# First expert layer: routing weights repeated over the partitions by transfers from a table in memory instead of by TensorE

## What is computed

```python
scores = jax.nn.sigmoid(x @ router_w.T)                 # 2048 tokens x 16 experts
_, topk_idx = jax.lax.top_k(scores + e_bias[None, :], TOP_K)   # TOP_K = 4
topk_w = jnp.take_along_axis(scores, topk_idx, axis=1)
topk_w = topk_w / (topk_w.sum(axis=-1, keepdims=True) + 1e-20)
combine = zeros((T, E)).at[arange(T)[:, None], topk_idx].add(topk_w)
# for each expert, with its column c of combine:
gu = x @ gu_w.T; g, u = jnp.split(gu, 2, axis=1)
acc + c[:, None] * (jax.nn.silu(g) * u @ d_w.T)
# and one shared expert without a weight
```

## Time and profile before

| | |
|---|---|
| median of 3 runs | 739.35 us |
| lowest, highest | 735.06, 740.98 us |
| time of the profiled execution | 740.54 us |
| its span in the profile | 738.8 us |
| mean granted clock of TensorE in it | 0.941 |

### The profile page before, as it was taken

One profiled execution on the slowest core, in us unless ns is written; L12 is line 12 of the kernel. 1 busy time (PEld: TensorE's weight loads), 2 busy tenths in 40 slices (PEclk: granted clock), 3 DMA queues, 4 the chain that ended last, 5 costly groups with the idle time before them and its releaser, 6 DMA issues.

```text
span 738.8 us, 14867 instructions
## 1 busy us (share of the span) xinstructions
PE 694.2 (94%) x4707; PEld 622.9 (84%) x4707; DVE 471.8 (64%) x1331; ACT 257.4 (35%) x484; POOL 356.1 (48%) x435
## 2 busy tenths in 40 slices
PE   4899999999999999998999984899999999999996
PEld 3758878888888888886677773799999999999995
DVE  4958597677777777775799958344544454454443
ACT  1355512333333333346466622222222232323221
POOL 6217693455446545549222034255354655465553
PEclk9786599999999999999899985899999999999999
DMA  9900103678877787769900047422425445434222
GB/s 220 343 3 1 58 0 122 236 247 271 264 242 257 262 265 248 248 230 430 367 20 31 31 138 267 147 44 41 154 45 151 97 122 155 151 75 135 44 37 22
DMA packets 60266, 114.96 MB, mean 156 GB/s; under 512 B 15185, under 2 KB 29394, under 8 KB 57778
## 3 DMA queue, kind: packets, MB, share of 16 engines
q1 hardware_dynamic: 50514, 103.48, 41.0%
q0 software_dynamic: 8736, 10.39, 8.5%
q10 hardware_dynamic: 960, 0.33, 0.2%
HBM read 68.89 MB, written 45.29 MB: 155 GB/s over the span
## 4 chain that ended last, share of the span: by engine, by line
PE 84%; DVE 10%; issue 3%; ACT 2%; DMA 1%; POOLq 0%; POOL 0%; DVEq 0%
PE ps L1114 19%; PE ps L1115 19%; PE ps L1116 19%; PE ps L1399 4%; PE ps L1244 2%; PE ps L1253 2%; PE ps L986 2%; PE ps L1290 2%; PE ps L1050 2%; PE ps L1041 2%; PE ps L1161 1%; PE ps L1266 1%; PE ps L1201 1%; PE ps L1378 1%; PE ps L1282 1%
## 5 line engine op out<-in xcount | busy, mean ns | idle before, releaser
L604 POOL TENSOR_TENSOR part_lo<-wexp,part_hi 128x256 fp32r<-128x256 f32 x136 | 104.8, 795 | 107.4 <-ACT part_hi L855 106.6
L715 POOL DMA_INDIRECT out_rows<-vbd,slot_row x39 | 63.3, 1623 | 105.6 <-DVE vbd L1947 74.0
L1114 PE MATMUL ps<-w_hi,x_high 128*128 x312 | 104.6, 335 | 1.1 <-DVE x_low L1952 1.1
L1115 PE MATMUL ps<-up_low,x_high 128*128 x312 | 101.1, 324 | 0.0
L1116 PE MATMUL ps<-w_hi,x_low 128*128 x312 | 101.0, 324 | 0.0
L1968 DVE TENSOR_TENSOR arena<-arena,ps 128x704 f32<-128x704 f32 x39 | 34.6, 888 | 102.5 <-ACT arena L954 102.5
L1114 PE MATMUL ps<-xn_high,gu_high 128*128 (+3 forms) x208 | 90.9, 437 | 0.0
L837 ACT ACTIVATE wexp<-ps 128x512 f32<-128x512 f32 (+1 forms) x52 | 31.1, 599 | 147.1 <-PE ps L1116 147.1
L1115 PE MATMUL ps<-xn_low,gu_high 128*128 (+3 forms) x208 | 81.9, 394 | 0.0
L1116 PE MATMUL ps<-xn_high,gu_low 128*128 (+3 forms) x208 | 81.7, 393 | 0.0
L954 ACT ACTIVATE arena<-ps 128x704 f32<-128x704 f32 x39 | 29.6, 760 | 119.1 <-PE ps L1116 119.1
(11 more groups left out here) (297 smaller groups left out, 1675.1 us busy)
## 6 DMA issues: line engine op xcount, KB each, us to landing
wexp<-in_wexp SPq DMA_DIRECT2D x68, 256.0 KB, 3.4
w_hi_rows<-part_hi SPq DMA_DIRECT2D x68, 256.0 KB, 3.1
w_lo_rows<-part_lo SPq DMA_DIRECT2D x68, 256.0 KB, 2.7
w_hi<-w_hi_rows SPq DMA_DIRECT2D x8, 2048.0 KB, 19.5
up_low<-w_lo_rows SPq DMA_DIRECT2D x8, 1408.0 KB, 6.0
down_low<-w_lo_rows SPq DMA_DIRECT2D x8, 768.0 KB, 8.3
wexp<-in_gu SPq DMA_DIRECT2D x2, 1632.0 KB, 11.2
xn_rows<-arena SPq DMA_DIRECT2D x8, 256.0 KB, 2.1
```

The source lines that it names most:

```text
L604: r = pool.tensor_tensor(part_lo[:, n % 2, some], part_w[:, n % 4, some], part_hi[:, n % 2, some].bitcast(F32), ALU.subtract)
L715: pool.indirect_dma_start(out=out_rows, out_offset=bass.IndirectOffsetOnAxis(ap=slot_row[:, i:i + 1], axis=0), in_=yb[:, i % 2, :], in_off ...
L1114: pe.matmul(out, high, rows_high, start=start, stop=False, skip_group_check=True)
L1115: pe.matmul(out, high, rows_low, start=False, stop=False, skip_group_check=True)
```

## The change

The three-part split and the spreading matmul go. The normalised weights `cw0` (fp32) of a group are transposed by one fp32 transpose into 64 rows (4 tiles of 16 experts), copied to `cT` by ACT, and stored by SP, in four transfers, as a table `cw_rows` of 16 experts by 2048 tokens in memory. For each chunk from 1 on SP issues two transfers, which read the two experts' rows of 512 tokens once for each partition, into one of four buffers `w_spread` in SBUF (256 KB in all for a chunk). DVE's multiplication by the weights waits for them and reads that buffer instead of PSUM. In SP's program the parts' loop is merged with these transfers.

```diff
+        w_spread = [view(wexp, at, 512) for at in (20416, 20928, 4096, 4608)]
+            def store_weights(first, groups):
+                for j in range(4):
+                    sp.dma_start(cw_v[:, first:first + groups, j, :],
+                                 cT[j * E0:(j + 1) * E0, first * P:(first + groups) * P].rearrange(
+                                     "e (g p) -> e g p", p=P)).then_inc(cw_stored, 16)
+
+            def load_weights(n):
+                g, c = n // (C0 - 1), chunk_of(n % (C0 - 1) + 1)
+                if n >= 4:
+                    sp.wait_ge(b_mult, n - 3)
+                sp.wait_ge(cw_stored, 16 * 8 if g else 16 * 4)
+                e = c * P // I0
+                edge = (e + 1) * I0 - c * P
+                for expert, lo, hi in ((e, 0, edge), (e + 1, edge, P)):
+                    sp.dma_start(w_spread[n % 4][lo:hi, :],
+                                 cw_rows[expert, g * 512:(g + 1) * 512].partition_broadcast(hi - lo)).then_inc(w_in[n % 4], 16)
...
+            sp.wait_ge(b_cT, 1)
+            store_weights(0, 1)
+            sp.wait_ge(x_new, XA)
+            for n in range(3):
+                load_part(n)
+            for n in range(3):
+                load_weights(n)
+            for g in range(NG):
+                for q in range(C0):
+                    if g == 0 and q == 10:
+                        sp.wait_ge(b_cT, 2)
+                        store_weights(1, NG - 1)
+                    n = g * (C0 - 1) + q + 2
+                    if q and n < NG * (C0 - 1):
+                        load_weights(n)
+                    for part in range(parts_by(g, q - 1), parts_by(g, q)):
+                        store_part(part)
...
-            pool.memset(spread, 0.0).then_inc(pool_step, 1)
-            v = spread.rearrange("p (e u) -> p e u", e=E0)
-            for part in range(3):
-                pool.wait_ge(pool_step, 10 + part)
-                pool.affine_select(out=v, in_=v, compare_op=ALU.not_equal, fill=1.0, base=-32 * part,
-                                   pattern=[[-1, E0], [0, I0]], channel_multiplier=1).then_inc(pool_step, 1)
...
-            pool.wait_ge(b_c3, 3)
+            pool.wait_ge(b_chosen, 1)
...
+            def copy_weights(first, groups):
+                act.wait_ge(b_turned, first + groups)
+                at = slice(first * P, (first + groups) * P)
+                act.activation(cT[:, at], bank(4)[0:4 * E0, at], ACT.Copy).then_inc(b_cT, 1)
+            copy_weights(0, 1)
...
-                        pe.matmul(bank(4), spread[:, chunk_of(c) * P:(chunk_of(c) + 1) * P], cT[:, bass.ds(g * 512, 512)],
-                                  start=True, stop=True).then_inc(b_spread, 1)
...
+                pe.transpose(bank(4)[0:4 * E0, g * P:(g + 1) * P], cw0[:, 4 * g:4 * g + 4, :].rearrange("p t e -> p (t e)"),
+                             ident[:, :]).then_inc(b_turned, 1)
 
             up0(0, 0, 0)
             pe.wait_ge(b_sig, 1)
+            pe.wait_ge(v_ready, B)
+            turn_weights(0)
             ffn0_group(0, 0)
...
                     if c:
-                        dve.wait_ge(b_spread, g * (C0 - 1) + c)
-                        dve.tensor_tensor(hm0[:, c % 2, :], hm0[:, c % 2, :], bank(4), ALU.mult).then_inc(b_mult, 1)
+                        dve.wait_ge(w_in[(c - 1) % 4], g * (32 * (C0 - 1) // 4) + 32 * ((c - 1) // 4 + 1))
+                        dve.tensor_tensor(hm0[:, c % 2, :], hm0[:, c % 2, :], w_spread[(c - 1) % 4], ALU.mult).then_inc(b_mult, 1)
```

More of the change, by code:

```diff
@@ L355, in program @@
         NG = NT // 4
-        weights5 = bank(5).bitcast(BF16)
-        WEIGHTS_AT = [bank(4).bitcast(BF16)[:, 0:512], weights5[:, 0:512], weights5[:, 512:1024], weights5[:, 0:512]]
+        w_spread = [view(wexp, at, 512) for at in (20416, 20928, 4096, 4608)]
+        w_in, cw_stored = [sem(f"w_in{n}") for n in range(4)], sem("cw_stored")
+        cw_rows = nc.dram_tensor("cw_rows", (E0, NT * P), F32, kind="Internal").ap()
         PIECE = 256
@@ L427, in load_part, with store_part @@
                 sp.dma_start(part_w[:, n % 4, :], w_flat[:, n * PART:(n + 1) * PART]).then_inc(p_in[n % 4], 16)
-            sp.wait_ge(x_new, XA)
-            for n in range(3):
-                load_part(n)
-            for n in range(NPART):
+            cw_v = cw_rows.rearrange("e (g t p) -> e g t p", t=4, p=P)
+            def store_weights(first, groups):
[13 more added lines that the diff above has]
+                                 cw_rows[expert, g * 512:(g + 1) * 512].partition_broadcast(hi - lo)).then_inc(w_in[n % 4], 16)
+            def store_part(n):
                 part = slice(n * PART, (n + 1) * PART)
@@ L1003, in _ @@
             pe.wait_ge(a_routed, 2)
-            pe.matmul(bank(7)[:, 0:NK], ones[0:1, :], brow, start=True, stop=True).then_inc(a_bias, 1)
+            pe.matmul(bank(7)[:, 0:NK], ones[0:1, :], brow, start=True, stop=True).then_inc(a_route, 1)
             def score_sets(b):
@@ L1154, in ffn0_group @@
                 for c in range(C0):
-                    if c:
-                        if k == 0 and c == 1:
-                            pe.wait_ge(b_cT, 1)
-                            pe.wait_ge(pool_step, 13)
-                        else:
-                            pe.wait_ge(b_mult, g * (C0 - 1) + c - 1)
-                        pe.matmul(bank(4), spread[:, chunk_of(c) * P:(chunk_of(c) + 1) * P], cT[:, bass.ds(g * 512, 512)],
-                                  start=True, stop=True).then_inc(b_spread, 1)
                     if c < C0 - 1:
                         up0(g, c + 1, k)
-                        if k == 0 and c == 0:
-                            turn_weights(0)
                         down0(g, c, k)
                     if k == 0 and c == 8:
-                        turn_weights(1)
-                        turn_weights(2)
-                    if k == 0 and c == 10:
-                        turn_weights(3)
+                        for later in range(1, NG):
+                            turn_weights(later)
                     if k and c in (8, 10):
@@ L1176, in turn_weights @@
             def turn_weights(g):
-                pe.wait_ge(b_c3, 6 if g else 3)
-                if g == 3:
-                    pe.wait_ge(b_cT, 3)
-                at = WEIGHTS_AT[g]
-                for j in range(4):
-                    mm = pe.transpose(at[0:96, j * P:(j + 1) * P], c3[:, 4 * g + j, :], identb[:, :])
-                mm.then_inc(b_turned, 1)
+                pe.wait_ge(b_chosen, 2 if g else 1)
+                pe.transpose(bank(4)[0:4 * E0, g * P:(g + 1) * P], cw0[:, 4 * g:4 * g + 4, :].rearrange("p t e -> p (t e)"),
+                             ident[:, :]).then_inc(b_turned, 1)
             up0(0, 0, 0)
             pe.wait_ge(b_sig, 1)
+            pe.wait_ge(v_ready, B)
+            turn_weights(0)
             ffn0_group(0, 0)
             pe.wait_ge(b_low, B)
-            pe.wait_ge(b_cT, NG)
             with pe.Fori(1, NG) as g:
@@ L1642, in _ @@
             chosen_scores(first).then_inc(b_step, 1)
+            dve.wait_ge(b_step, 4)
+            dve.tensor_reduce(sums[:, first], cw0[:, first, :], AX.X, ALU.add).then_inc(b_step, 1)
             dve.wait_ge(b_step, 5)
[L1644 removed]
+            dve.tensor_scalar(sums[:, first], sums[:, first], 1e-20, None, ALU.add).then_inc(b_step, 1)
             dve.wait_ge(b_step, 6)
[L1646 removed]
+            dve.reciprocal(recs[:, first], sums[:, first]).then_inc(b_step, 1)
             dve.wait_ge(b_step, 7)
[L1648 to L1659 removed]
+            normalised(first).then_inc(b_chosen, 1)
             def select_rest(q):
```

87 lines of the change are left out of this document (24 added, 63 removed).

## The result

The changed kernel took 744.84 us (median of 20 runs, 737.52 to 750.86), the kernel before 738.08 beside it (20 runs): a ratio of 1.0091, 95% interval 1.0061 to 1.0121. That is 6.8 us slower, where the forecast was 1.55 us slower; 745 lies in the range of 731 to 748. The profiled execution has a span of 745.8 us against 738.8.

The account below looks back on a forecast made before the run. PE was taken to bound the kernel, busy 210.2 of 211 us from 115 to 326 us. The terms -1.1 + 1.45 - 10.3 + 11.5 = +1.55 us gave 741 us on the median's scale, range 731 to 748.

Parts of the forecast that it names:

- The spreads, -10.3: On PE, 44 spreading matmuls of 0.235 us each go: -10.3 us.
- The port, +11.5: DVE's multiplication, now with two SBUF inputs, takes turns with POOL; PE stalls 0.67 us in 15 two-part chunks: +11.5 in all.
- The ladder: In two-part chunks DVE and POOL take turns, so the second subtraction ends 5.11 us after the silu, 4.67 before.
- Rivals 2 and 5: Port stalls in two-part chunks: 2, only 0.1 us, 729 to 734, chance 0.20; 5, 0.9 us, 746 to 747, chance 0.07.
- The trade of the two: In the chunk loop, saved spreads of -10.3 us against port stalls of +11.5 us come out about even.
- the likeliest case: Rival 1, the even trade of spreads against port stalls in the chunk loop: 736 to 746 us, chance 0.48.
- The hand-over, +1.45: At the stage's start, the first weights go through memory and land at 100.2 us: +1.45 us, between 0 and 5.
- Rival 4: At the stage's start, the hand-over takes 5 us and the clock falls to 1.2 GHz behind the gap: 747, chance 0.13.
- The program's start, -1.1: Without POOL's selects, DVE's first tensor_scalar, which PE waits for, ends about 1.1 us earlier: -1.1, 0 to -1.3.
- The later store, 0: Group 0, chunk 10: table stores hold SP some 3 us, covered by 3 chunks of weights and 3 parts in hand: 0.
- Traffic, hidden: From 115 to 326 us, 44 chunks of 256 KB raise the DMA share from 0.74 to 0.91, still hidden.
- a rival by bytes, 756: Rival 3: repeated reads of one row cost twice a part's bytes, so the DMA queue becomes the bound: 756, chance 0.12.

Follow-up runs that it names:

- Both taken away: Changed kernel with weight transfers of 16 columns instead of 512 from the fifth chunk on, and the multiplication's operand read from PSUM: 726.06 us, 0.9851.
- small loads: Changed kernel with each weight transfer bringing 16 columns instead of 512 from the fifth chunk on, all transfers and waits kept: 739.82 us, 1.000.
- the same edit alone in the kernel before: Kernel before, with POOL building the 0/1 matrix after the first layer's powers instead of before them: 741.38 us, 1.0065.
- the high store first: Changed kernel with weights issued behind each chunk's parts and each high store ahead of the load three parts on: 737.68 us, 1.000.

## Why the prediction was right and where it was not

*The spreads, -10.3.* Both taken away, groups 1 and 2 take 56.5 and 56.1 us instead of 58.5 and 58.6: 2.0 and 2.5 for 12 spreads, 0.17 to 0.21 each, against 0.235. Where nothing else waits the price is exact: the three steps from silu 5 to silu 8 of group 0 take 4.41 us each in the kernel before and 4.18 or 4.19 in the changed one, 0.23 less.

*The port, +11.5.* The difference of the two runs with small loads is 229.6 - 222.3 = 7.3 us by the sums and 11 by the ratios, so the term was right or a little large. The ladder was right to 0.1 us in the chunk above and in 9 more of the 15; 10 x 0.67 = 6.7 us would be its part in that run (an estimate). In the changed kernel itself it is mostly absent: POOL starts late because ACT is late, most multiplications of groups 1 to 3 take 0.69 to 0.9 us and not 1.13, and only 3 of the 15 chunks end beyond 5.0 us after their silu. Without POOL at work the multiplication takes 0.69 us, not the 0.6 of the forecast. Rivals 2 and 5 were bounds on either side and neither came.

*The trade of the two*, even by the forecast (+1.2), was even: 1.000 with small loads. That is why the forecast for the whole was near. That the measured 745 lies in the range is luck for the rest: nothing in the sum or in the 736 to 746 of the likeliest case stands for the loop of the stores, and the part of the range above it was put there for other causes.

*The hand-over, +1.45.* The timeline of the changed kernel, SP, ACT, DVE and one row of PE:

```profile
88.22 0.22 DVE L1631 TENSOR_TENSOR arena<-arena,recs 128x64 f32<-128x64 f32 x1
89.87 1.28 ACT L863 ACT_TABLE_LOAD   x1
89.88 1.71 SPq L430 DMA_DIRECT2D cw_rows<-arena  x4
91.16 0.59 ACT L863 ACTIVATE wexp<-ps 96x512 f32<-96x512 f32 x1
91.63 1.38 SPq L425 DMA_DIRECT2D wexp<-in_wexp  x3
93.05 6.81 SPq L442 DMA_DIRECT2D wexp<-cw_rows  x10
94.02 0.35 PE L1135 MATMUL ps<-dn_high,h_high 96*128 96x256 f32 x1 [1.71 <-DVE h_low L1710]
97.53 1.21 DVE L1701 TENSOR_TENSOR wexp<-wexp 128x512 f32<-128x512 f32 x1 [1.39 <-DMA wexp<-cw_rows]
```

From the normalised weights (88.44) to the first multiplication 9.1 us go by; the forecast had 8.4 (91.8 to 100.2). The way over memory was priced well: the stores landed 1.3 to 1.4 us after their issue and the first two loads 3.6 and 3.9, where the forecast had 2.1 and 3.4. By the fit of the Trainium skill, "DMA: Bandwidth & Descriptors", section "Anatomy of one DMA" (about 2.0 us fixed, for transfers issued by GpSimd), the two trips are 4 us; the trace has less for the first and nearly twice as much for the second, which had three loads of parts ahead of it.

What was not seen is on ACT. Up0 of chunk 0 ends at 89.43, and silu 0 could start; but the copy now stands ahead of it, and behind the copy the load of ACT's table (1.28 us). In the kernel before that load was over while ACT waited for up0:

```profile
88.97 1.28 ACT L837 ACT_TABLE_LOAD   x1
93.00 0.59 ACT L837 ACTIVATE wexp<-ps 96x512 f32<-96x512 f32 x1 [2.76 <-PE ps L1116]
```

So silu 0 starts 1.7 us late, at 91.16, and PE stands idle for 1.71 us before down0 of chunk 0, where it was 0.34 before. Behind this gap the clock fell, once and briefly:

```profile
94.90:98.40 3.50, 3.50 (x13) 3.02 (x13) 2.11 (x3) 0.00 (x0) 3.50 (x6) 0.51 0.75 241
```

3.5 us at 1.2 GHz hold 1.75 us of products, so this costs 1.75. Rival 4 had priced such a fall, behind a longer gap in which PE waits for the transfers. That gap is not what came first: the clock fell at about 94.8, and DVE's 1.39 us of waiting for the weights ended at 97.53, when it was already low. The fall is there behind silu 0 in all twelve profiled kernels with the change, whose gap on PE is 1.7 to 2.2 us, and in neither of the two without it, whose gap is 0.34 and 0.24 us.

From the end of up0 of chunk 0 to silu 5 the kernel before takes 22.5 us and the changed one 25.1. So the term of 1.45 was 2.6, inside its bounds of 0 and 5; without the clock's 1.75 it would have been 0.9. This part of the loss would go, as far as the timeline shows, with the table's load or the copy moved; no run tries it.

*The program's start, -1.1.* The line got quicker and PE began 0.7 us earlier (11.69 instead of 12.42); no gain at the end is shown, and the same edit alone in the kernel before came out slower.

*The later store, 0.* This was wrong. The timeline of SP and ACT at chunk 10 of group 0:

```profile
136.68 1.84 SPq L430 DMA_DIRECT2D cw_rows<-arena  x4
139.77 0.78 SPq L442 DMA_DIRECT2D wexp<-cw_rows  x2
...
141.06 0.43 SPq L450 DMA_DIRECT2D w_hi_rows<-part_hi  x1
...
146.46 0.63 ACT L876 ACTIVATE part_hi<-wexp 128x512 fp32r<-128x512 f32 x1 [5.34 <-DMA w_hi_rows<-part_hi]
147.00 0.58 ACT L863 ACTIVATE wexp<-ps 128x512 f32<-128x512 f32 x1
```

The cover that was named, three parts and three chunks of weights in hand, covers loads. The high store was not in it: it stood behind, at 141.06, and silu 12 came 6.48 us after silu 11 (140.52) instead of 4.65 as in the kernel before: some 1.8 us. With the high store first it comes after 4.73, so this too is the order.

*Traffic, hidden.* This is the step that failed, and the forecast is too low because of it. The share was forecast at 0.91 and was 0.88, and the queue was, as forecast, not full. But the step asked only whether the bytes fit (and priced a rival by bytes, 756), and whether ACT "idles about 3 us in a chunk". The idle time was not free: ACT has two buffers, and a part's loop is copy, issue, landing, next copy but one. The added transfers lengthened mostly the landing (3.0 to 4.9 us on the average) and little the time from the copy to the issue (0.62 to 0.76, though more in single chunks, as where SP issues 0.85 us of weights and 0.44 of a load ahead of the store). In a chunk with two parts both turns of that loop lie ahead of the next silu. It cost 7.1 us beyond the even trade. The sentence that ACT's idle time "covers stores that land a microsecond later" failed on both counts: they land 1.9 us later, and the copies, with 1.7 us of waiting for them before, have 112.7. The forecast followed what stands behind the weights on their queue, and never asked what stands behind them in SP's order for ACT's sake.

## What to carry to other kernels

When transfers are added to a queue that other engines wait on, price them by the loop that they stand in (issue order, landing, number of buffers) and not by the queue's share; issue first what frees a buffer, and last what is needed a few steps later. In the table of waits add up all rows of the instruction that is late, for one wait can stand under several names (here half of it under "issue"), and look for the wait that shows the bound (here ACT for PE) and whether it comes back. When an instruction is moved ahead of another on an in-order engine, ask what else moves with it (here a table's load that had been hidden). Costs on two engines that feed the same product overlap, so mending either one alone may show little.

## What was not expected of the hardware

A store of 256 KB landed 3.1 us after its issue at a DMA share of 0.74 and 4.9 us at 0.88, well before the DMA engines were full. Reading one row of memory 32 to 96 times cost about what a part's bytes cost: 44 GB/s more took 0.14 more of the share, where 246 GB/s take 0.74. A gap of 1.7 us on PE stood before a fall of the clock to 1.2 GHz for some 3.5 us. And the granted clock between 60 and 86 us differed between executions of programs that are the same up to there (0.50 and 0.74), which moved the start of this stage by some 5 us; differences of that size between two single profiles say nothing.
